# One of four attention heads is turned in 32-blocks by VectorE and regrouped through DRAM; TensorE turns the other three

## What is computed

```python
# layer 1: a decoder layer, 16 heads of 32 channels
ln_out = layernorm(x, ln1_s, ln1_b)
q, k, v = split(ln_out @ w_qkv + b_qkv)
x = x + merge(attention(q, k, v, mask_1)) @ w_ao + b_ao          # self-attention
q = layernorm(x, ln2_s, ln2_b) @ w_q + b_q
k, v = split(context @ w_kv + b_kv)
x = x + merge(attention(q, k, v, mask_2)) @ w_co + b_co          # cross-attention
x = x + gelu(layernorm(x, ln3_s, ln3_b) @ w1 + b1) @ w2 + b2     # perceptron, width 2048
# layer 2: a non-local block on the result, with 1x1 convolutions theta, phi, g, w
# attention(q, k, v, mask):
scores = (q @ k.T) / sqrt(32); scores = scores * mask - 10000 * (1 - mask)
probs  = softmax(scores)                                          # 256 x 256 for each head
out    = probs @ v
```

## Time and profile before

| what | value |
|---|---|
| time, median of 3 runs | 2041.2 us (2039.52 to 2042.16) |
| span of the profiled execution | 2038.2 us |
| PE, VectorE (DVE), ScalarE (ACT) busy, whole span | 2018.1, 1447.7, 1166.7 us |
| DMA engines' share in use | 32.5% by the main queue |
| instructions | 41730 |

### The profile page before, as it was taken

How to read it: one execution, slowest core, us unless ns; L and a number is a source line. 1 busy time by engine, 2 the same in 40 slices (tenths; PEclk the granted TensorE clock), 3 DMA queues, 4 the chain that set the end, 5 groups by cost and what they waited for, 6 DMA issues and landing times. The chain is left out here.

```text
span 2038.2 us, 41730 instructions
## 1 busy us (share of the span) xinstructions
PE 2018.1 (99%) x14096; PEld 1621.0 (80%) x14096; DVE 1447.7 (71%) x3874; ACT 1166.7 (57%) x3239; POOL 450.6 (22%) x434
## 2 busy tenths in 40 slices
PE   9999999999999999999999999999999999999998
PEld 8877777777777777777777776788888888888887
DVE  7798988888889888888888898565344443435333
ACT  4388888888888888787788888522111121212111
POOL 1011111111113242222232233053031331313000
PEclk9999999999999999999999999999999999999999
DMA  8513243243144344344334334432212212121201
GB/s 270 171 35 77 83 119 77 64 113 97 48 141 133 109 134 109 85 121 126 86 111 123 95 108 120 138 99 70 80 33 77 46 62 72 41 77 46 64 24 47
DMA packets 332469, 190.25 MB, mean 93 GB/s; under 512 B 210688, under 2 KB 276864, under 8 KB 332288
## 3 DMA queue, kind: packets, MB, share of 16 engines
q1 hardware_dynamic: 332288, 187.97, 32.5%
HBM read 137.00 MB, written 50.86 MB: 92 GB/s over the span
## 5 line engine op out<-in xcount | busy, mean ns | idle before, releaser
L1279 ACT ACTIVATE A_p<-A_p,A_nmax 128x256 f32<-128x256 f32 x1024 | 509.1, 506 | 0.0
L1564 DVE TENSOR_TENSOR A_p<-A_sc,A_mk 128x1024 f32<-128x1024 f32 x256 | 312.7, 1221 | 109.1 <-PE A_tp L1046 108.9
L1574 DVE CUSTOM_DVE_ANT_0 A_p<-A_p,A_ma 128x256 f32<-128x256 f32 x1024 | 374.5, 423 | 5.2
L1285 ACT ACTIVATE A_pt<-A_tp 128x512 f32<-128x512 f32 x512 | 276.9, 592 | 142.2 <-PE A_tp L1046 141.8
L1046 PEld LDWEIGHTS A_tp<-A_ident,A_p 128*128 128x128 f32 x2048 | 230.1, 141 | 71.8 <-issue 44.1
L1046 PE MATMUL A_tp<-A_ident,A_p 128*128 128x128 f32 x2048 | 274.2, 277 | 2.0 <-ACT A_pt L1285 1.6
L1279 ACT ACTIVATION_READ_ACCUMULATOR A_p<-A_p,A_nmax 128x1 f32 x1024 | 202.8, 198 | 0.0
L1414 ACT ACTIVATE A_mk<-A_tp,A_cols 128x512 f32<-128x512 f32 x62 | 42.7, 689 | 269.0 <-PE A_tp L68 269.0
L766 POOL TENSOR_TENSOR A_res<-A_res,A_o_bias 128x512 f32<-128x512 f32 x64 | 84.9, 1338 | 473.1 <-DVE A_nmax L1574 281.3
L1414 ACT ACTIVATE A_ma<-A_tp,A_cols 128x512 f32<-128x512 f32 x62 | 42.8, 690 | 242.4 <-PE A_tp L68 242.4
L66 PE MATMUL A_banks<-A_xt_h,A_w_h 128*128 128x512 f32 x384 | 161.3, 420 | 0.9 <-DVE A_res L1543 0.5
(11 more groups left out here) (245 smaller groups left out, 4856.4 us busy)
## 6 DMA issues: line engine op xcount, KB each, us to landing
...
A_rt<-inverses SPq DMA_DIRECT2D x512, 32.0 KB, 1.8
...
turned<-A_x SPq DMA_DIRECT2D x240, 64.0 KB, 2.3
inverses<-A_turned_inv SPq DMA_DIRECT2D x512, 1.0 KB
A_e<-ctx_t SPq DMA_DIRECT2D x16, 512.0 KB, 3.9
A_xt_l<-turned SPq DMA_DIRECT2D x16, 512.0 KB, 4.0
```

Of the source, the lines that this page charges most:

```text
L1279: act.activation(p[:, g % 2, j, t, :], p[:, g % 2, j, t, :], ACT.Exp, scale=-1.0, bias=nmax[:, g % 2, j, t:t + 1], accum_out=rsum[:, g % 2 ...
L1285: act.activation(pt[:, j, :, :], tp[:, j % 2, :].rearrange("p (c s) -> p c s", c=TPB), ACT.Copy)\
L1564: dve.tensor_tensor(p[:, g % 2, heads, :, :].rearrange("p j t s -> p j (t s)"), sc[:, heads, :], m, ALU.mult)\
L1574: dve.tensor_tensor_reduce(out=a_, in0=a_, in1=ma[:, b, t, :], scale=-1.0, scalar=BIG, op0=ALU.add, op1=ALU.min, accum_out=nmax[:, g % 2, ...
```

## The change

A constant `MOVED = 1` says how many of a group's four heads go another way; `TURNS` is then 3.

- For head 0 VectorE transposes the exponentials in place in blocks of 32x32, one instruction on 128x512 values (`exponentials_in_blocks`), placed in its slot between `scaled` and the first `maxima`. It waits for the head's two exponentials.
- SP stores the head to a new DRAM buffer in four DMAs, each of 32 partitions in pieces of 32 values (128 bytes), 64 KB each (`store_exponentials`). They stand between `store_inverses` and `load_inverses` (in slot 6 behind the loads L494).
- At the start of the next slot SP loads the head back, 256 KB in pieces of 128 values, into `pt[:, 0]` (`load_exponentials`), after a wait for the stores and for the `weigh` of the slot before.
- TensorE's `turn` runs for heads 1 to 3: two at the slot's start, one at the second place. ScalarE's `turned_out` runs three times instead of four. `weigh` also waits for the load, and reads head 0 through an access pattern of two pieces.
- VectorE's `mask_scores` of heads 0 and 1 waits for the stores of the slot before and for one turn, where it waited for two turns.
- ScalarE takes the two exponentials of head 0 at the start of its slot, ahead of `turned_out`.

The diff, without the passing on of names:

```diff
@@ -25,6 +25,8 @@
 CI = 128
 EPS = 1e-5
 BIG = 3.0e38
+MOVED = 1
+TURNS = HPG - MOVED
 DMA = 16
 
 
...
@@ -538,6 +541,28 @@
                     own = inv_dram[g % 2].rearrange("(t j) s -> j t s", j=HPG)[j:j + 1]
                     sp.dma_start(rt[rr, :].rearrange("p (t s) -> p t s", t=TPB), own.broadcast_to([HD, TPB, P]))\
                         .then_inc(ld_i, DMA)
+
+            def store_exponentials(r, h):
+
+                grp, _, g = group(r, h, 0)
+                sp.wait_ge(p_blk, grp + 1)
+                wait(sp, ld_p, (grp - 1) * DMA)
+                keys = p_dram[g % 2].rearrange("j t (b i) q -> i (j t b) q", i=32)
+                for n in range(P // 32):
+                    rows_ = slice(n * 32, (n + 1) * 32)
+                    own = p[rows_, g % 2, 0:MOVED, :, :].rearrange("i j t (b q) -> i (j t b) q", q=32)
+                    sp.dma_start(keys[:, :, rows_], own).then_inc(st_p, DMA)
+
+            def load_exponentials(r, h, pv):
+
+                grp, _, g = group(r, h, -1)
+                if grp == 0:
+                    sp.wait_ge(w_lo, 3 * KT)
+                else:
+                    sp.wait_ge(done, pv[1])
+                sp.wait_ge(st_p, (grp + 1) * (P // 32) * DMA)
+                sp.dma_start(pt[:, 0:MOVED, :, :].rearrange("p j a (b q) -> p (j a b) q", q=P),
+                             p_dram[g % 2].rearrange("j t (c p) q -> p (j t c) q", p=P)).then_inc(ld_p, DMA)
 
             def load_raw(c, some=range(KT)):
                 for t in some:
@@ -596,10 +621,14 @@
 
             def slot(r, k, h, a_, b_, own, pv):
                 if own:
+                    load_exponentials(r, h, pv)
                     store_inverses(r, h)
                     if h == 6 and 0 < k < NU:
                         for t in range(2):
                             load_res(k - 1, r - 1, t + 2)
+                if exists(k, h, 0):
+                    store_exponentials(r, h)
+                if own:
                     load_inverses(r, h)
                 if h == 0 and k > 1:
                     for t in range(2):
@@ -1032,32 +1061,38 @@
                                              start=(n == 0), stop=(n == 2))
                 last.then_inc(scored, 1)
 
-            def turn(r, k, h, j):
+            def turn(r, k, h, i):
                 grp, _, g = group(r, h, -1)
-                if NG * k + h - LAG - 1 == 0 and j == 0:
+                n, j = grp * TURNS + i, MOVED + i
+                if grp == 0 and i == 0:
                     pe.wait_ge(pgt_ok, B)
                     pe.wait_ge(m1_ok, B)
                 pe.wait_ge(exped, grp * HPG * TPB + (j + 1) * TPB)
-                wait(pe, pt_ok, grp * HPG + (j - 1))
-                if j < 2 and h in (0, 7) and k == (h == 0):
-                    pe.wait_ge(x_lo, (r + (h == 7)) * TT + (j + (3 if h == 0 else 1)))
+                wait(pe, pt_ok, n - 1)
+                if i < 2 and h in (0, 7) and k == (h == 0):
+                    pe.wait_ge(x_lo, (r + (h == 7)) * TT + (n % 2 + (3 if h == 0 else 1)))
                 for t in range(TPB):
                     for c in range(TPB):
-                        last = pe.transpose(tp[:, j % 2, c * S + t * P:c * S + (t + 1) * P],
+                        last = pe.transpose(tp[:, n % 2, c * S + t * P:c * S + (t + 1) * P],
                                             p[:, g % 2, j, t, c * P:(c + 1) * P], ident[:, :])
                 last.then_inc(turned, 1)
+
+            def turned_keys(j, c):
+
+                return pt[:, j, :, c * P:(c + 1) * P] if j < MOVED else pt[:, j, c, :]
 
             def weigh(r, h, bank):
                 grp, blk, g = group(r, h, -1)
                 b, f = g // KT, g % KT
                 occupy(bank, cx_ok, NG, h - LAG, r)
-                pe.wait_ge(pt_ok, (grp + 1) * HPG)
+                pe.wait_ge(pt_ok, (grp + 1) * TURNS)
+                pe.wait_ge(ld_p, (grp + 1) * DMA)
                 pe.wait_ge(v_ok, blk * TT + (b + 1) * TPB)
                 for c in range(TPB):
                     for j in range(HPG):
                         rr = slice(j * HD, (j + 1) * HD)
                         last = pe.matmul(banks[rr, bank, 0:S], v[:, b * TPB + c, f * P + j * HD:f * P + (j + 1) * HD],
-                                         pt[:, j, c, :], start=(c == 0), stop=(c == TPB - 1))
+                                         turned_keys(j, c), start=(c == 0), stop=(c == TPB - 1))
                 last.then_inc(done, 1)
 
             def before():
@@ -1106,8 +1141,8 @@
                 if early[0] is not None:
                     hidden(0, early[0], True)
                 if own:
-                    turn(r, k, h, 2)
-                    turn(r, k, h, 3)
+                    for i in range(2, TURNS):
+                        turn(r, k, h, i)
                 if early[1] is not None:
                     hidden(0, early[1], True)
                 unit_step(a_, r, k, 3)
@@ -1116,7 +1151,7 @@
                 if k == 0 and h == 0:
                     chain_2(B - 1)
                 if even is not None:
-                    pe.wait_ge(pt_ok, group(r, h, -1)[0] * HPG + 4)
+                    pe.wait_ge(pt_ok, (group(r, h, -1)[0] + 1) * TURNS)
                     turn_rows(r + (k < NU), even, tp[:, 0, :])
                     turn_rows(r + (k < NU), odd, tp[:, 1, :])
                 unit_step(b_, r, k, 2)
@@ -1151,7 +1186,7 @@
                 if first and f < KT:
                     pe.wait_ge(masked, 2 * GROUPS)
                 elif first and f < EARLY:
-                    pe.wait_ge(pt_ok, GROUPS * HPG)
+                    pe.wait_ge(pt_ok, GROUPS * TURNS)
                 else:
                     pe.wait_ge(h_act, n - 1)
                 cols_ = slice(f % KT * P, (f % KT + 1) * P)
@@ -1279,10 +1314,11 @@
                 act.activation(p[:, g % 2, j, t, :], p[:, g % 2, j, t, :], ACT.Exp, scale=-1.0,
                                bias=nmax[:, g % 2, j, t:t + 1], accum_out=rsum[:, g % 2, t, j:j + 1]).then_inc(exped, 1)
 
-            def turned_out(r, h, j):
+            def turned_out(r, h, i):
                 grp, _, g = group(r, h, -1)
-                act.wait_ge(turned, grp * HPG + (j + 1))
-                act.activation(pt[:, j, :, :], tp[:, j % 2, :].rearrange("p (c s) -> p c s", c=TPB), ACT.Copy)\
+                n = grp * TURNS + i
+                act.wait_ge(turned, n + 1)
+                act.activation(pt[:, MOVED + i, :, :], tp[:, n % 2, :].rearrange("p (c s) -> p c s", c=TPB), ACT.Copy)\
                     .then_inc(pt_ok, 1)
 
             def weighed(r, k, h):
@@ -1344,23 +1380,24 @@
                 if k == NB + 1 and h == 0:
                     act.wait_ge(y_ok, NB * TT)
                 bare = k == NU and h < 2
+                first = TPB * MOVED
+                if now:
+                    for n in range(first):
+                        exponential(r, h, n)
                 if own:
-                    for j in range(HPG if bare else 2):
-                        turned_out(r, h, j)
-                if now:
-                    exponential(r, h, 0)
-                    exponential(r, h, 1)
+                    for i in range(TURNS if bare else 2):
+                        turned_out(r, h, i)
                 if leaves and not late(k, h):
                     weighed(r, k, h)
+                if now:
+                    exponential(r, h, first)
                 if own and not bare:
-                    turned_out(r, h, 2)
-                    turned_out(r, h, 3)
-                if now:
-                    exponential(r, h, 2)
+                    for i in range(2, TURNS):
+                        turned_out(r, h, i)
                 unit_out(a_, k)
                 if now:
-                    exponential(r, h, 3)
-                    exponential(r, h, 4)
+                    for n in range(first + 1, 5):
+                        exponential(r, h, n)
                 if even is not None:
                     rows_turned(r + (k < NU), even, tp[:, 0, :])
                     rows_turned(r + (k < NU), odd, tp[:, 1, :])
@@ -1559,7 +1596,10 @@
                         dve.wait_ge(m_ok, blk * 2 - (14 - b))
                     else:
                         dve.wait_ge(m_ok, 1)
-                wait(dve, turned, (grp - 2) * HPG + 2 * (part + 1))
+                if heads.start < MOVED:
+                    wait(dve, st_p, (grp - 1) * (P // 32) * DMA)
+                if heads.stop > MOVED:
+                    wait(dve, turned, (grp - 2) * TURNS + heads.stop - MOVED)
                 m = mk[:, b, :, :].rearrange("p t s -> p (t s)").unsqueeze(1).to_broadcast([P, 2, TPB * S])
                 dve.tensor_tensor(p[:, g % 2, heads, :, :].rearrange("p j t s -> p j (t s)"), sc[:, heads, :], m, ALU.mult)\
                     .then_inc(masked, 1)
@@ -1582,6 +1622,13 @@
                     .then_inc(inv_ok, 1)
                 wait_apart(dve, inv_ok, grp + 1, st_i, (grp - 1) * (P // 32) * DMA)
```

(12 more changed lines are left out.)

3 lines of the change are left out of this document (2 added, 1 removed).

## The result

The changed kernel takes 2131.2 us (median of 4 runs, 2130.9 to 2137.8), before 2041.1 us (4 runs, 2039.5 to 2042.2): a ratio of 1.0447, 95% interval 1.0431 to 1.0463. It is 90 us slower. The forecast was 2078 us, in a range of 2016 to 2114: the sign and the place were right, the size was not.

A forecast was written before the change was run, and what follows sets the result against it. TensorE was taken to bound the kernel, with VectorE and SP's queue near their limits. Fourteen bodies at 2.9 us more, 41 us, less 4 us elsewhere, added 37 to 2041.2: 2078 us, range 2016 to 2114.

The forecast's parts named there:

- TensorE's gain: One head's four transposes fewer on TensorE in each group: 0.40 us, so slots it bounds go from 9.30 to 8.90.
- TensorE stays the only bound: Rival, chance 0.04: every slot gains TensorE's 0.40 us, 128 times, 51 us in all, giving 1990 us.
- VectorE's price: The added block transpose costs VectorE 0.62 us a slot, making slots 0, 1 and 3 9.40 us long.
- VectorE bounds four slots: Rival, chance 0.20: SP's queue holds, slots 4 to 6 take 26.8 us, a body 73.1, giving 2019 us.
- The queue sets slot 6: SP's late queue makes VectorE's first instruction of slot 7 wait 3 to 4 us for slot 6's head stores.
- VectorE's delay: VectorE's first instruction of slot 7 waits for head stores landing at 877.1, where it could begin at 872.8.
- The size of that chain: SP's queue from slot 4 to slot 6's head stores landing: slots 4 to 6 take 31.0 us instead of 27.9.
- the queue is worse: Rival, chance 0.16: longer tile and head stores start slot 7 2.6 us later again, giving 2114 us.
- slots 7, 0 to 3, against before: The five other slots of a body, each at its larger bound: 46.3 us where they took 46.5.
- The ends: The other 16 groups, pipeline ends and body 15, give back 0.25 us each, 4 us in all.
- The longest chain that I allowed: SP's queue in slots 4 to 6 at its slowest: 14 times 5.5 us, 77, less 4, giving 2114 us.

The follow-up runs named there:

- e1: The changed kernel without head 0's block transpose, stores, load and the waits for them; TensorE still turns three heads: 1995.0 us.
- e2: The changed kernel with VectorE's block transpose kept, but without head 0's stores and load: 2024.7 us.
- e7: The changed kernel, with VectorE transposing head 0 into buffers of their own from body 10 on, so the mask no longer waits for head stores: 2128.0 us.
- e11: The kernel before, with four more 64 KB stores in 128-byte pieces after each slot's inverse stores, into a tensor nobody reads: 2099.5 us.
- e6: The changed kernel without the sixteen block stores of x in bodies 2 to 14, the loads kept: 2046.5 us.
- e12: The changed kernel with the four block stores of x tile 0 issued in slot 3 instead of slot 4: 2101.8 us.
- e3: The changed kernel with the same five transfers a group, but a sixteenth of the stores' bytes and a load of 32 pieces: 2093.9 us.
- e8: The changed kernel without head 0's load and the wait for it, the stores kept: 2095.8 us.

## Why the prediction went as it did

**TensorE's gain: 0.40 us a slot: right.** In e1 slots 0 to 6 are 0.35 to 0.44 us shorter, 0.40 on average. The mean over all slots is 0.35 only since slot 7 gains nothing: there VectorE waits for the inverses, behind SP's queue. The rival "TensorE stays the only bound" missed that, even for a change that would cost VectorE nothing: it said 1990, and e1 took 1995.0.

**VectorE's price: 0.62 us; slots 0, 1 and 3 at 9.40.** The transpose is listed with 0.70 us, but the next instruction starts 0.62 after it (933.45, 934.07), so the price held. Slots 0, 1 and 3 came out at 9.3 in e2; in the changed kernel their means are 9.41, 9.66 and 9.48, with single bodies up to 11.7 us. Slot less idle time overstates VectorE's work: neighbouring instructions overlap by 0.08 us (933.45 + 0.70 against 934.07), an instruction after an idle gap does not, so that closing the gap gains some 0.08 more: 8.78 + 0.62 − 0.08 = 9.32, which is an estimate from these rows. The rival "VectorE bounds four slots" gave 2019. With the transfers away e2 took 2024.7, its slot 7 again with the wait for the inverses.

**The queue sets slot 6: right, but not through one wait alone.** The first mask of slot 7 waits for the head stores, at the place of the text, and longer than its 3 to 4 us: 4.7 to 7.7. The text had `weigh`'s wait for its load inside VectorE's delay. In five of 14 bodies it is the chain through `weigh` that the profile names, and e7 shows that it holds slot 6 near 14 us by itself. That the earlier trace rows leave too little waiting time to fill is shown in three ways: four stores a slot added to the kernel before cost 59 us (e11), slot 6 is back at about 9.3 us once sixteen others are gone (e6), and four moved out of the stretch give 0.51 us each (e12).

**The size of that chain: wrong, and this is the step that failed.** From the start of slot 4 to the start of slot 7 I had put 31.0 us, as 6.8 to the start of slot 4's tile stores, 22.3 from there to the end of slot 6's head stores, and 1.9 to land. The means over 14 bodies are 7.7, 23.8 and 2.1, in sum 33.6, as by VectorE's slots. Group by group, each from its start to the start of the next:

| group of SP's queue, us | forecast | measured, mean |
|---|---|---|
| slot 4, inverse loads | 1.8 | 2.4 |
| slot 4, eight tile stores | 4.2 | 4.9 |
| slot 5, inverse stores | 2.6 | 1.5 |
| slot 5, load of x, eight tile stores, two finished tiles | 6.5 | 7.6 |
| all the rest, the landing among it | 15.9 | 17.1 |

The three groups of head stores are not among the causes: 1.97, 1.95 and 2.15 us for the 2.05 to 2.1 of the text. I had read nearly every duration from one body of the kernel before. Over its 14 bodies the eight tile stores of slot 4 take 4.6 us where my row had 4.2, the run of slot 5 (without the load of x) takes 6.5 where it had 5.85, and the inverse stores of slot 5 take 1.45 where it had 2.63, the longest of the 14; these three errors nearly cancel. So the choice of the body does not explain the missing 2.6 us. What the sum had at nothing, without a reason, is that groups already there get longer with the change: from the kernel before to the changed one the inverse loads of slot 4 go from 1.7 to 2.3 us, the run of slot 5 from 6.5 to 7.1. About 0.1 us between one group and the next, which I had counted only in places, adds up as well. For the inverse loads e3 shows the bytes of the head to be the cause, since there they take 1.8 us; the run of slot 5 takes 7.0 in e3 too, and why it is longer stays open.

The rival "the queue is worse" put slots 4 to 6 at 33.6 us with a chance of 0.16, and that is what they took. Half of this is luck: it had 1.2 us more for the eight tile stores, where 0.7 came, and 1.35 us more for the head stores, where nothing came. It fell short at the ends, as the forecast did. The whole sum, term by term:

| term, us | forecast | measured |
|---|---|---|
| slots 4 to 6, against before | +3.1 | +5.6 |
| slots 7, 0 to 3, against before | −0.2 | +0.1 |
| 14 bodies | +41 | +79 |
| the rest of the run (the other 16 groups among it) | −4 | +11 |
| sum | +37 | +90 |

**The ends: −4 us, measured +11: the second term that failed.** I counted there only TensorE's gain. In the drain nothing else is left to do between the stores and the load of a head: VectorE's mask, ScalarE's exponentials, the block transpose, four stores, a landing, a load and its landing follow one another. Slots 0 and 1 of body 16 take 12.0 and 10.6 us, where before they took 7.3 and 8.4. Body 15 is 3.8 us longer too; what holds it was not followed. The window of the two slots of body 16 in the changed kernel, and the two waits of PE in them:

```profile
1338.40:1361.00 22.60, 10.34 (x98) 7.00 (x99) 14.59 (x48) 10.78 (x38) 3.47 (x3) 0.64 0.66 166
```

```profile
1347.29 1.94 PE L1094 MATMUL A_banks<-A_pt,A_v 128*32 128x256 f32 x16 [4.37 <-DMA A_pt<-exponentials]
...
1357.88 1.93 PE L1094 MATMUL A_banks<-A_pt,A_v 128*32 128x256 f32 x16 [3.60 <-DMA A_pt<-exponentials]
```

e8, without the load, has these two slots at 9.7 and 7.9 us.

**The range.** The longest chain that I allowed ended at 2114, with the ends still at a gain. The bodies as measured and the ends at −4 would have given 2116, at its edge; the 15 us between the ends' −4 and +11 carry the result well out of it.

**Left open.** Why in one body the inverse loads of slot 4 are the long group (3.2 us in body 9) and in another the tile stores (5.4 in body 13); e3 shows that fewer bytes make issues shorter, not which transfer holds up which issue. No run parts the sixteen tile stores' bytes from their issues. Why e2's slot 7 varies from 9.1 to 11.0 us beyond its wait for the inverses was not followed.
